# Cross attention with key blocks taken in batches of 3, 3, 3 and 4 in place of 2 each

## The reference, cut to what matters

```python
# x: (1, 2048, 256); ctx_1024: (1, 1601, 256)
x = x + self_attention(layernorm(x))          # 16 heads of 16, causal, alibi bias
x = x + cross_attention(layernorm(x), ctx)    # 16 heads of 64, below
x = x + fp8_feed_forward(layernorm(x))

# cross attention, query = layernorm(x)
q = (query @ Wq + bq).reshape(1, 2048, 16, 64)
k = (ctx @ Wk + bk).reshape(1, 1601, 16, 64)
v = (ctx @ Wv + bv).reshape(1, 1601, 16, 64)
scores = einsum('bqhd,bkhd->bhqk', q, k) / 8
out = einsum('bhqk,bkhd->bqhd', softmax(scores), v).reshape(1, 2048, 1024)
out = out @ Wo + bo + query                   # then a layer norm with gamma, beta
```

## Time and profile before

| | us |
|---|---|
| median of 3 runs | 1935.51 |
| lowest and highest run | 1913.4, 1937.34 |
| span of the profiled execution | 1916.1 |
| PE busy over the span | 1767.4 (92%) |
| DVE, ACT, POOL busy | 1270.0, 920.3, 940.8 |

### The profile page before, as it was taken

One profiled execution on the slowest core, in us unless ns is written; L12 is line 12 of the kernel. 1 busy time (PEld: TensorE's weight loads), 2 busy tenths in 40 slices (PEclk: granted clock), 3 DMA queues, 4 the chain that ended last, 5 costly groups with the idle time before them and its releaser, 6 DMA issues.

```text
span 1916.1 us, 29762 instructions
## 1 busy us (share of the span) xinstructions
PE 1767.4 (92%) x10698; PEld 885.2 (46%) x10698; DVE 1270.0 (66%) x2503; ACT 920.3 (48%) x1866; POOL 940.8 (49%) x800
## 2 busy tenths in 40 slices
PE   7999989998988999999999999999999999999983
PEld 3544444443444544445545545544554554554431
DVE  5677777777643657756656655665665675667888
ACT  2345676666665243344454444445445444445441
POOL 1000000000001466658888888898888888882111
PEclk9867999999999899999999999999999999999996
DMA  4232113332011000000000000000000000000001
GB/s 115 34 37 35 21 16 36 36 45 55 2 34 55 11 0 1 1 11 4 1 11 4 1 10 4 1 11 1 4 11 1 4 1 1 4 11 23 1 28 38
DMA packets 29129, 34.48 MB, mean 18 GB/s; under 512 B 4290, under 2 KB 27139, under 8 KB 27523
## 3 DMA queue, kind: packets, MB, share of 16 engines
q1 hardware_dynamic: 28984, 32.59, 9.1%
HBM read 14.99 MB, written 4.19 MB: 10 GB/s over the span
## 4 chain that ended last, share of the span: by engine, by line
PE 76%; DVE 16%; ACT 4%; issue 3%; SPq 1%; DMA 1%; POOL 0%; ACTq 0%; DVEq 0%; POOLq 0%
PE psum L974 17%; PE psum L954 14%; PE psum L939 9%; DVE maxima L1247 8%; PE psum L860 8%; PE psum L772 6%; PE psum L810 4%; PE psum L835 4%; PE psum L1005 3%; PE psum L927 3%; PE psum L872 2%; PE psum L986 2%; DVE parts_room L1341 1%; DVE stack_room L1297 1%; ACT stack_room L1116 1%
## 5 line engine op out<-in xcount | busy, mean ns | idle before, releaser
L1247 DVE TENSOR_REDUCE maxima<-psum 128x1 f32<-128x400 f32 (+5 forms) x1664 | 860.1, 580 | 322.7 <-PE psum L939 211.7
L747 POOL TENSOR_TENSOR parts_room<-parts_room,weights_room 128x512 f32<-128x512 f32 (+1 forms) x565 | 706.1, 1283 | 136.3 <-ACT weights_room L1137 136.3
L1137 ACT ACTIVATE weights_room<-psum 128x512 f32<-128x512 f32 (+1 forms) x757 | 405.5, 599 | 491.2 <-PE psum L954 429.4
L1065 ACT ACTIVATE weights_room<-psum 128x512 f32<-128x512 f32 (+3 forms) x640 | 300.2, 535 | 183.4 <-PE psum L835 104.1
L1455 POOL TENSOR_SCALAR rstd<-meanvar 128x2 f32<-128x2 f32 (+1 forms) x24 | 9.8, 408 | 726.9 <-DVE meanvar L1197 726.9
L954 PE MATMUL psum<-stack_room,dk_hi 64*128 64x512 f32 (+1 forms) x1408 | 264.1, 410 | 8.1 <-ACT weights_room L1137 4.8
L939 PE MATMUL psum<-k_later,stack_room 64*128 64x400 f32 (+1 forms) x896 | 243.4, 412 | 22.3 <-DVE stack_room L1297 14.6
L939 PEld LDWEIGHTS psum<-k_later,stack_room 64*128 64x128 f32 x896 | 128.4, 184 | 220.8 <-issue 121.2
L974 PE MATMUL psum<-weights_room,parts_room 128*64 128x512 f32 (+1 forms) x754 | 203.1, 606 | 0.0
L974 PE MATMUL psum<-weights_room,late_room 128*64 128x512 f32 (+1 forms) x760 | 202.5, 605 | 0.0
L835 PE MATMUL psum<-stack_room,stack_room 51*128 51x512 f32 (+3 forms) x640 | 143.4, 448 | 34.2 <-DVE maxima L1247 31.7
(11 more groups left out here) (136 smaller groups left out, 1854.4 us busy)
## 6 DMA issues: line engine op xcount, KB each, us to landing
stack_room<-parts_room SPq DMA_DIRECT2D x84, 128.0 KB
x_block<-x_dram SPq DMA_DIRECT2D x8, 512.0 KB, 4.8
x_middle<-x_block SPq DMA_DIRECT2D x4, 512.0 KB, 3.1
x_block<-x_middle SPq DMA_DIRECT2D x4, 512.0 KB, 3.9
out_dram<-x_block SPq DMA_DIRECT2D x8, 256.0 KB, 2.1
stack_room<-parts_room SPq DMA_DIRECT2D x24, 64.0 KB
parts_room<-ctx_dram SPq DMA_DIRECT2D x1, 1536.0 KB
stack_room<-shift_rows SPq DMA_DIRECT2D x64, 2.0 KB
```

The source lines that it names most:

```text
L747: engine.tensor_tensor(sum_[:kw, :], old[:kw, :], weights[u % NP_WEIGHTS][:kw, :], ALU.add) \
L1065: engine.activation(w_self[s % NW][:, m, 0:n], bank_of(use + m)[:, 0:n], ACT.Exp, scale=SELF_SCALE).then_inc(emptied(use + m), 1)
L1137: engine.activation(weights[u % NP_WEIGHTS][:kw, :], pair_scores[u % NSCORES][:kw, :], ACT.Exp, scale=CROSS_SCALE).then_inc(pair_exp, 1)
L1247: engine.tensor_reduce(maxima[:, p % 2, i // TB, n, i % TB, ch:ch + 1], bank_of(use + n)[:, 0:real - k0], AX.X, ALU.max) \
```

## The change

`pair_sweep2` takes the blocks of keys in batches of 3, 3, 3 and 4. After each batch of S it puts all V that are pending but for the newest one (`kept=1`), and after the last batch of a block of queries all of them (`kept=0`). A block of queries becomes S0 S1 S2, V0 V1, S3 S4 S5, V2 V3 V4, S6 S7 S8, V5 V6 V7, S9 S10 S11 S12, V8 V9 V10 V11 V12: 4 batches, 17 steps in `main`, 68 for a pair in place of 80. `spread` and `interleave` are unchanged and divide the same side work over the new list. `pass_step` is still called once for each V.

```diff
+BATCHES = (3, 3, 3, NS - 9)
...
-    def pair_values(self):
-        for _ in range(len(self.pending) or 1):
+    def pair_values(self, kept=0):
+        due, self.pending = self.pending[:len(self.pending) - kept], self.pending[len(self.pending) - kept:]
+        for _ in range(len(due) or 1):
             self.pass_step()
-        for p, b, j, s in self.pending:
+        for p, b, j, s in due:
             self.put("pair_values", p, b, j, s)
...
-        self.pending = []
...
     def pair_sweep2(self, p):
-        batch = []
-
         def scores(b, j):
             self.put("pair_scores", p, b, j, self.step)
-            batch.append((p, b, j, self.step))
+            self.pending.append((p, b, j, self.step))
             self.step += 1
-
-        def values():
-            self.pair_values()
-            self.pending, batch[:] = list(batch), []
 
         steps = []
         for b in range(NB):
-            for j0 in range(0, NS, 2):
-                steps += [(1, lambda b=b, j=j: scores(b, j), b) for j in range(j0, min(NS, j0 + 2))]
-                steps.append((min(NS, j0 + 2) - j0, values, b))
+            j0 = 0
+            for n in BATCHES:
+                steps += [(1, lambda b=b, j=j: scores(b, j), b) for j in range(j0, j0 + n)]
+                j0 += n
+                steps.append((n, lambda kept=int(j0 < NS): self.pair_values(kept), b))
         return steps
```

## The result

| | before | after |
|---|---|---|
| median of 4 runs beside each other | 1925.08 | 1961.51 |
| lowest and highest | 1913.4, 1937.34 | 1949.96, 1971.92 |
| ratio after to before (95% interval) | | 1.0209 (1.0158 to 1.0259) |
| span of the profiled execution | 1916.1 | 1947.9 |

The change makes the kernel 2.1% slower (1.6 to 2.6%). The forecast was 1930 and no change that counts; the median lies 3.5 us above the range.

A forecast was written before the change was run, and what follows sets the result against it. PE was taken to bound p = 1 to 6. Terms of -24 - 4 + 23 + 4 there, -2 in p = 0 and +10 in p = 7 gave +7 on 1916.1, some 1923; forecast 1930 for the median's level, range 1897 to 1958.

The forecast's parts named there:

- Doubled places: p = 1 to 6: two c directly behind V wait for DVE's reduces, 0.63 us each, 36 times, 23 us lost.
- Gain 3 x 0.33 = 1.0 us a block, 24 us over the 24 blocks of p = 1 to 6: PE: a round from S to V and back costs 0.33 us; a block has 4 in place of 7.
- queries: p = 1 to 6: V0 V1 come between each pair's first projection of queries and its c, 4 us gained.
- rival 4: PE's changes of shape cost the same since projections already part the rounds; only losses stand, +31, 1947; chance 0.08.
- The term for longer runs: p = 1 to 6: longer runs of c and S go at DVE's pace, 4 us lost on 24 blocks, 0 to 8.
- The exponentials: p = 1 to 6: third and fourth S waiting for ACT cost 0, up to 10 us over all as upper end.
- -2 us for three blocks, from -5 to +8: p = 0: blocks with 32 c, three or four c in a row behind V, go from 41.3 us to 40.6.
- p = 7: Last pair: 3 us lost by exponentials less rounds, 7 by sums waiting for DVE's adds; +10, from 0 to +20.
- POOL: End of a block: POOL's adds fall back three steps but hold nothing up; free, at most 1 us a block.
- Exponentials of V12: End of a block: V12 stands behind its own S12, four V ahead cover its exponentials; free.
- Rival 2: Slower by the ring of three banks for c: full 0.85 for each c c run, +39, 1955 or 1974; chance 0.11.
- Rival 1: Rounds decide: 0.45 us a round gained, c c paid back inside the run, -28, 1888 or 1908; chance 0.22.

The follow-up runs named there:

- e1: Kernel before, with side work of p = 1 to 6 doubled at the first and ninth step of each block as in the change: 1939.33 us, ratio 1.0102.
- e3: Kernel after, with the eight doubled places of each pair moved so that no c c comes directly behind V: 1940.08 us, ratio 1.0087.
- e11: e8 with e10's edit and exponentials for half of the queries in all but the first uses: 1864.33 us, one run.
- e12: e9 with the exponentials halved as in e11: 1841.92 us, one run.
- e8: e3's kernel with DVE's maximum over only the first half of each chunk of keys: 1888.53 us, one run.
- e9: Kernel before with DVE's maximum over only the first half of each chunk of keys: 1859.89 us, one run.
- e13: e9 repeated with more runs: 1868.12 us, ratio to before 0.9735.
- e2: Kernel after, with the load of the tail's weights put ahead of the last block's shift rows on SP: 1963.73 us, ratio to before 1.0224.
- e4: Kernel after, with p = 7 alone in batches of 2: 1949.69 us, ratio to before 1.0128.
- e5: Kernel after, with p = 0 alone in batches of 2: 1959.24 us, ratio to before 1.0195.
- e10: e7 with the last block's shift rows six passes behind a pair's last maxima in place of three: 1915.75 us, ratio to before 0.9962.
- e7: The change in p = 1 to 6 only, with e2's and e3's edits: 1916.29 us over 12 runs, ratio to before 0.9982.

## Why the prediction was wrong

The profile moved by 31.8 us where +7 was forecast. Of the 24.8 between them, in like terms, 13.5 lie in p = 1 to 6 (rounds that bring too little), 6.4 in p = 0, 9.6 in p = 7 (above all the late load), and -4.7 is the start's scatter.

**Doubled places: right.** c c falls behind V as the prediction placed it, L937 waits 12.2 us where some 12 were foretold, and it costs 0.60 to 0.61 where 0.63 was said. e1 puts it in alone (21.6 us with the projection at the border) and e3 takes it out (22.0): nearly all of the 23 us.

**The first failed step: "Gain 3 x 0.33 = 1.0 us a block, 24 us over the 24 blocks of p = 1 to 6".** The batches brought -9.5 us there (e3), where -24 was forecast for rounds, queries and runs together. The price of a round wasn't what failed. It was read in p = 7, on the bare round of the earlier trace rows, and beside side steps e11 and e12 show 0.40. What failed is the count, and a term put at nothing. A round was taken to be two changes of shape, but projections stand between S and V in many places, and a pair in e3 has 18 changes fewer, not 24. At 0.20 for one change (half of the 0.40) that is 1.2 us a pair that stays, an estimate. That is rival 4's argument, to which I gave 0.08; it holds for a quarter of the changes and not for all. And the turn of the maxima and the projection by Wo take 9.2 us a pair in e3 where they took 8.1 before, by the same adding up: 1.0 us a pair, six in all, for waits that stand in no term (L824's 1.3 is one of them). DVE's pace has the rest: with it c and S together are 0.1 us a pair shorter in e3 than before, without it (e11 and e12) 1.4. The term for longer runs, 4 us over all, was too small for this by about half. Roughly then, for a pair: -4.0 forecast, 0.8 more gained by the price of 0.40, and 1.2, 1.0 and 0.6 not gained, -2.0 for the -1.7 measured. These parts overlap, and no run takes just one of them away.

The exponentials cost nothing that shows as long as DVE sets the pace: no wait of L954 for L1137 is listed in that pair of e3. Freed of DVE the third and fourth S do wait (e8), and halving the exponentials helps only the larger batches. So 0 was right for this kernel as far as its waits show, and would be wrong for one with a faster maximum.

The Trainium skill, TensorEngine Tiling (Array Packing), Key Properties, says that changing the tiling mode drains TensorE. The 0.33 of the earlier trace rows and the 0.40 of e11 and e12 agree that a change costs something. The same page's PSUM Bottleneck, which I weighed as speaking against the change, is borne out: its price in c c was measured, and in e9 and e13 a pair with half the work of emptying is 6.6 us shorter.

**The second: the queue of SP was not walked.** The prediction counted POOL's and DVE's queues past the moved V, but `pass_step` moves SP's stages as well. `pair_rows` of the last block went ahead of `tail_weights_load`, 7.5 us in the first block of p = 7 (e2, and e4 from the other side). It was to be seen in the list: five passes in one call reach `ROWS_LAG`, and SP's next stage is the tail's load.

**The third: p = 0, "-2 us for three blocks, from -5 to +8".** It became +7.1 in the profile, and 5 to 11 over the pairs of profiles; 2.7 us of the 7.1 are the projection and the V that lie inside the border now. Two things were wrong. The sum of c runs doesn't follow from its own rule: with 32 c, n - 0.5 for each run, 0.855 for each V and 0.15 for each batch, seven batches come to 40.7 us and four to 41.7, so the rule foretold a loss of 1 us a block and not a gain of 0.7. And it had no term for the clock, which was 0.95 for 0.97, with four c in a row behind V. e5 confirms the place (196.7) and shows that nearly half of it comes back in p = 1. With half the maxima, where the clock stays at 1.00 in both, p = 0 takes 176.4 us in threes (e8) and 174.9 in twos (e9), less than the 2.7 of the border: there, without the fall of the clock, the threes cost nothing.

**p = 7: right in size, +10.9 against +10** (e4), in part by luck. Both of its parts are in the trace: 0.6 lost at the third S, and the sums held by DVE's adds, 13.7 us in three blocks against 5.6 in two before. But the first three blocks lose 18.7 us together and the last gives 7.8 back, where the sum had some 10 for the former and nothing for the latter. A piece left out is DVE's own wait for the copy of those sums, 30.4 us for 18.3. The 18.7 of the whole region are the 10.9 and the late load.

**POOL: free, as said.** 127.09 us a pair, and nothing shows L1135 held by it. **Exponentials of V12: free** too. **The new wait at L824**, 1.3 us a pair, stands in no term; moving it gained 0.1 (e10), as the next wait took its place.

**The rivals.** Rival 2 gave 1955 and 1974, and the result lies between, but its cause is not what happened: c c cost 22, not 31, and the rest is SP's queue, the clock in p = 0, and rounds that bring too little. Rival 1 had nearly the right price of a round, 0.45 for the 0.40 of e11 and e12, and the gain that it built on it didn't come. In rival 2, three rounds a block are 24 us against 36 doubled places, which balance at 0.67 us a place and not at four fifths; and the run c c S c S c S c has three more c behind the first two, not four, so its 0.85 stands within 0.05.

**The level.** I put 7 of the 19 us between profile and median on top. The median of before beside after was 1925, 9 above its span, so this came out; three runs couldn't tell it from 0 or 19, so it was a lucky choice in part. 31.8 in the profile became 36 in the medians.

## What to carry to other kernels

When an order is written out as one list, a change that bunches passes moves the stages of every queue: list, for each queue (the DMA issuers too), what now stands ahead of each stage that occurs once, because a load behind a waiting copy is late by the whole wait. A price read where two steps stand bare beside each other can hold elsewhere, but count how often it will be saved: where side work parts the steps, fewer rounds are not as many fewer changes of shape, and stages that once stood far behind what they need come close to it. When an engine is paced by a ring that another empties, look at its weight loads too: in p = 3 PE itself lists no wait for the maxima, its weight loads 6.8 us, and half the emptying gained 6.6 (and 20.7 in p = 0, part of it the clock). Shortening the emptying can pay more than any reordering.

## What the runs showed of the hardware that I had not expected

**A small DVE instruction held by POOL.** In e1 a sum over 128x1 elements on DVE took 4.61 us, where the trace after has 0.16 for the same instruction:

```profile
1741.98 4.61 DVE L1360 TENSOR_TENSOR norm_room<-norm_room 128x1 f32<-128x1 f32 x1
```

```profile
1741.59 1.27 POOL L747 TENSOR_TENSOR parts_room<-parts_room,parts_room 128x512 f32<-128x512 f32 x1
1742.82 1.29 POOL L1493 TENSOR_TENSOR parts_room<-parts_room,parts_room 128x512 f32<-128x512 f32 x1
1744.07 2.50 POOL L747 TENSOR_TENSOR parts_room<-parts_room,weights_room 65x512 f32<-65x512 f32 x2
```

It ends at 1746.59, POOL's last add at 1746.57. It is the first step of the tail's weights, and the first block of p = 7 took 30.4 us in e1 for 26.0 in before, whose batches are the same. The other runs with twos in p = 7 and no late load sort by it. Where the instruction takes 0.37 to 0.43 us (before, e7, e10), the block takes 25.4 to 26.0 and PE doesn't wait in it. Where it takes 4.6 to 6.8 (e1, e9, e12, e13), the block takes 30.4 to 31.0, and PE waits 1.9 to 3.1 us for ACT, at a clock of 0.94 or 0.95. In e13:

```profile
1672.94 6.79 DVE L1360 TENSOR_TENSOR norm_room<-norm_room 128x1 f32<-128x1 f32 x1
```

No run moves only this instruction, so that it costs the 5 us rests on these seven profiles. The Trainium skill, SBUF — State Buffer, SBUF: two separate sides, says that a DVE instruction with two SBUF inputs and a GpSimd instruction that reads SBUF contend for a shared pair of ports, which the first to start holds for its whole instruction while the other is blocked. This trace agrees that DVE is blocked, but the block lasts here over four instructions of POOL.

**The clock gives a stall a second price.** After the 4.74 us in which PE idled in p = 7, the block ran at 0.91 of full clock: 4.74 us of idle time and 7.5 us lost. PE was busy for 34.25 us in that block and for 31.32 with the same matmuls in e2, at 1.00.
